# Top-2 experts computed for sorted rows instead of for all rows, beside a recurrent scan

## The reference

```python
xn = layernorm(x)
# L0_attn: a recurrence along the 512 tokens of every sequence
x_norm = layernorm(xn) * g + b;  x_norm += depthwise_conv3(x_norm)
gate, input_gate = split(x_norm @ gate_w.T + gate_b)      # 2 x 128 columns
Bm = x_norm * sigmoid(input_gate) @ B_w.T + B_b           # 64 columns
Cm = x_norm @ C_w.T + C_b
def step(state, bc):                                      # lax.scan, 512 steps
    s = layernorm(state @ A_bar + b_t);  return s, c_t * s
s = (ssm @ D_w.T + D_b) * sigmoid(gate)
# L0_ffn: a dense part and a mixture of 8 experts, of which each row uses 2
abel_out = gelu(xn2 @ abel_w + abel_b)
topw, topi = top_k(xn2 @ moe_gate_w + moe_gate_b, 2);  topw = softmax(topw)
h  = gelu(xn2 @ ew1[e] + eb1[e])                          # 128 -> 256, every e
eo = h @ ew2[e] + eb2[e]                                  # 256 -> 128, every e
moe_out = sum_e eo * w_dense[e];  moe_out = moe_out @ expm(gens[i]) for i in 0, 1, 2
gate = sigmoid(concat(abel_out, moe_out) @ gc_w + gc_b)
ffn = xn + abel_out * (1 - gate) + moe_out * gate
out = x + s * silu(ffn)
```

## Time and profile before

| | us |
|---|---|
| median of 3 runs | 539.81 (539.56 to 542.43) |
| profiled execution, its own time | 543.42 |
| profiled execution, span in the trace | 541.6 |
| front, to the first transpose of the scan | 102.79 |
| scan, 5 rounds | 402.3 (102.79 to 505.10) |
| behind the scan | 36.5 |

### The profile page before, as it was taken

One profiled execution on the slowest core, in us unless ns is written; L12 is line 12 of the kernel. 1 busy time (PEld: TensorE's weight loads), 2 busy tenths in 40 slices (PEclk: granted clock), 3 DMA queues, 4 the chain that ended last, 5 costly groups with the idle time before them and its releaser, 6 DMA issues. The chain is left out here.

```text
span 541.6 us, 13237 instructions
## 1 busy us (share of the span) xinstructions
PE 444.0 (82%) x4780; PEld 343.0 (63%) x4780; DVE 377.2 (70%) x1471; ACT 250.1 (46%) x597; POOL 209.2 (39%) x201
## 2 busy tenths in 40 slices
PE   2866799799889888988898898689889889998247
PEld 1766748477656666676676676567766566776135
DVE  3878579377878587777768676667677576868445
ACT  0325922445455335554455546154645355554420
POOL 2266645012532253243325414332443143425443
PEclk9959959899999798999999999799999799999759
DMA  8200000000000000000000000000000000000004
GB/s 268 79 7 0 2 1 1 2 1 2 2 2 2 1 2 1 1 2 1 2 2 0 3 1 1 2 1 2 1 2 2 1 1 2 2 1 2 0 4 155
DMA packets 6483, 7.65 MB, mean 14 GB/s; under 512 B 2424, under 2 KB 4378, under 8 KB 6426
## 3 DMA queue, kind: packets, MB, share of 16 engines
q1 hardware_dynamic: 5850, 4.77, 2.8%
q10 hardware_dynamic: 576, 2.10, 1.1%
HBM read 4.76 MB, written 2.10 MB: 13 GB/s over the span
## 5 line engine op out<-in xcount | busy, mean ns | idle before, releaser
L1336 POOL TENSOR_TENSOR xpad<-xpad 128x512 f32<-128x512 f32 x64 | 82.8, 1294 | 243.0 <-ACT xpad L1248 187.3
L1157 PE MATMUL bank<-ew,hT 128*128 128x128 f32 x1024 | 143.5, 289 | 0.0
L1248 ACT ACTIVATE xpad<-bank,wd 128x128 f32<-128x128 f32 x256 | 73.1, 369 | 128.4 <-PE bank L1157 128.2
L1157 PEld LDWEIGHTS bank<-ew,hT 128*128 128x128 f32 x1024 | 124.8, 195 | 9.1 <-issue 0.7
L1240 ACT ACTIVATE hT<-bank,eb_col 128x512 f32<-128x512 f32 x128 | 81.2, 687 | 50.7 <-PE bank L194 50.7
L980 PE MATMUL bank<-Mrep,wT 32*32 32x64 f32 x2560 | 69.7, 223 | 36.4 <-DVE wT L886 35.8
L980 PEld LDWEIGHTS bank<-Mrep,wT 32*32 32x32 f32 x2560 | 45.0, 106 | 77.8 <-issue 72.4
L896 DVE SCALAR_TENSOR_TENSOR ring<-bank,Rho,Dv 128x64 f32<-128x64 f32 x124 | 35.2, 284 | 65.1 <-PE bank L980 61.5
L192 PE MATMUL bank<-xf,ew_high 128*128 128x512 f32 x128 | 61.6, 481 | 0.0
L194 PE MATMUL bank<-xf,ew_rest 128*128 128x512 f32 x128 | 52.2, 408 | 0.0
L193 PE MATMUL bank<-xf,ew_high 128*128 128x512 f32 x128 | 52.2, 408 | 0.0
(11 more groups left out here) (288 smaller groups left out, 716.5 us busy)
## 6 DMA issues: line engine op xcount, KB each, us to landing
X<-in_L_attn_x ACTq DMA_DIRECT2D x4, 512.0 KB, 6.1
out<-gi SPq DMA_DIRECT2D x8, 256.0 KB, 2.0
late<-in_L_ffn_ew SPq DMA_DIRECT2D x1, 1024.0 KB, 5.3
pulled<-in_L_ffn_gens SPq DMA_DIRECT2D x1, 192.0 KB
gate_w<-in_L_attn_gate_w SPq DMA_DIRECT2D x1, 128.0 KB, 7.4
D_w<-in_L_attn_D_w SPq DMA_DIRECT2D x2, 32.0 KB, 6.4
abel_in<-in_L_ffn_abel_w SPq DMA_DIRECT2D x1, 64.0 KB, 1.8
bias_in<-in_L_ffn_abel_b SPq DMA_DIRECT2D x3, 0.5 KB
```

The costliest lines, as they stand in the source:

```text
L1157: t = pe.matmul(bE[e % 2][:, s * P:(s + 1) * P], hT[:, e % 2, k, s * P:(s + 1) * P], ew2[:, e, k, :], start=(k == 0), stop=(k == K - 1))
L1248: t = act.activation(scaled[e % 2][:, s, :], bE[e % 2][:, s * P:(s + 1) * P], ACT.Copy, scale=w)
L1336: pool.tensor_tensor(acc, acc, scaled[e % 2], ALU.add).then_inc(sem("added"), 1)
```

## The change

Instead of all 8 experts for all rows, only the two experts of each row are computed.

1. Routing makes places as well as weights: for both halves of the rows (2048 rows, 4096 row-expert pairs each), the pairs are sorted by expert, each expert's rows padded to full tiles of 128. A half has room for 39 tiles, both have 78. `slots` is each pair's place, `expert_of` each tile's expert.
2. GpSimd scatters the normalised rows by `slots` to DRAM: 64 indirect DMAs of 128 rows of 512 bytes (L1487). Later it gathers the results back: 64 indirect DMAs of 128 rows of 516 bytes (L1500). GpSimd has no arithmetic in the scan any more; the sorted buffers are cleared by two DMAs in the front.
3. A tile's weights (both matrices, bias, 581 words on 128 partitions, 297 KB) are copied from `experts` in SBUF to one of five `record` places by a DMA whose source is chosen by a register that SyncE loads (`fetch`, L1524), 78 of them. Rows come in and go out in three chunks per body of 13 tiles.
4. TensorE's program is loops. Round 0 is a loop of 8 turns of 4 steps, which carry `abel_pre`, `gate_pre` and a transposition of the result. Rounds 1 to 3 are 3 x 2 bodies of 16 steps with 13 tiles each: in step i it computes `layer1` of tile i-2, transposes the rows of tile i and computes `layer2` of tile i-3. Round 4 is a loop of 8 turns of 4 steps with three dummy products per step (`keep_warm`).
5. The split into high and rest parts is gone; the expert products are float32. C is projected in step 1 of each body.
6. The mixing of the results moves from GpSimd to VectorE, in given steps of the scan (from step 100 of 160 on, two of the eight tiles behind the scan), with ScalarE making the gains.
7. There is one block instead of three. The work behind the scan starts before the verdict of the check; the fallback would redo it.

```diff
+        HALF_TILES = Q * P * 2 // ROWS + E - 1      # 39
+        BODY = 13
+        experts = sb("experts", [P, E, RECORD])
+        record = sb("record", [P, 5, RECORD])
...
-                def split_tile(n):
-                    pool.wait_ge(sem("zT_used"), n + 1)
-                    split(xf[:, 0, n, :], xf[:, 1, n, :], gi[:, n, :])
...
+            dve.tensor_tensor_scan(places..., restart..., hits..., 0.0, ALU.mult, ALU.add)
...
+                def layer1(b, tile0, u):
+                    ...
+                    for k in range(K):
+                        t = pe.matmul(hidden_bank(u)[:, k * P:(k + 1) * P], w[:, k * P:(k + 1) * P], rows_T[:, u % 2, :], start=True, stop=True)
+                def layer2(b, tile0, u):
+                    ...
+                    for k in range(K):
+                        pe.matmul(o, hidden[:, u % 2, k, :], w[k], start=(k == 0), stop=False)
+                    pe.matmul(o, ones_all3[:, :], bias, start=False, stop=True).then_inc(sem("rows_done"), 1)
+                def keep_warm(times, bank=7):
+                    for i in range(times):
+                        pe.matmul(banks[bank][:, :], ones_all3[:, :], bias_all3[:, 1]..., start=True, stop=True)
...
-                for r in range(ROUNDS):
-                    for k in range(L):
-                        tensor_step(pe, r * PER + k + 1)
-                        n, i = divmod(r * L + k, TILE_STEPS)
-                        for h in range(...):
-                            expert_half(n, h)
+                with pe.Fori(0, NB) as n:
+                    tensor_step(pe, n * 4 + 1)
+                    abel_pre(n)
+                    tensor_step(pe, n * 4 + 2)
+                    gate_pre(n)
+                    tensor_step(pe, n * 4 + 3)
+                    tensor_step(pe, n * 4 + 4)
+                    abel_transposes(n)
+                with pe.Fori(0, 3) as r:
+                    with pe.Fori(0, 2) as h:
+                        for i in range(BODY_STEPS):
+                            tensor_step(pe, turn + (PER + i + 1))
+                            if 2 <= i < BODY + 2: layer1(b, tile0, i - 2)
+                            if i < BODY: rows_transpose(b, tile0, i)
+                            if i >= 3: layer2(b, tile0, i - 3)
+                            if i == 1: C_proj(2, b)
+                            keep_warm(FILL_BODY.get(i, 0))
+                with pe.Fori(0, L // 4) as j:
+                    for i in range(4):
+                        tensor_step(pe, j * 4 + (4 * PER + i + 1))
+                        keep_warm(3)
...
-                    act.copy(acc, bR4).then_inc(sem("sum_started"), 1)      # and scale(e), 8 per tile
+                for b in range(BODIES):
+                    for s in range(BODY_STEPS):
+                        gelus(b, s - 2); rows_transposed(b, s); rows_copied(b, s - 3)
+                        scalar_mix(...)        # ACT_MIX = {91: 0, 98: 1, 105: 2, 113: 3}
...
-                        pool.tensor_tensor(acc, acc, scaled[e % 2], ALU.add).then_inc(sem("added"), 1)
+                            pool.indirect_dma_start(sorted_rows[h], ...slots[:, j, q:q + 1]..., z_rows[:, q, :], None)
+                            pool.indirect_dma_start(pulls[:, n % 3, j, s, :], None, expert_rows[...], ...slots...)
...
+                    e = sp.value_load(expert_of[t:t + 1, h:h + 1], min_val=0, max_val=E - 1)
+                    if before >= 0:
+                        sp.wait_ge(sem("rows_done"), before + 1)
+                    sp.dma_start(record[:, at], experts[:, ds(e, 1), :].squeeze(1)).then_inc(sem(f"record{at}"), 16)
```

More of the change, by code:

```diff
@@ L17 @@
 UNROLL = 8
+ROWS = 128
+HALVES = 2
 SEG = 16
@@ new lines, in layer2 @@
+                def layer2(b, tile0, u):
+                    _, w, _, bias = fields(record[:, RECORD_PLACE[u]])
+                    pe.wait_ge(sem("hidden"), tile0 + (u + 1))
+                    pe.wait_ge(sem("rows_copied_out"), tile0 + (u + 1 + BODY - SINCE[u]))
+                    o = out_bank(u)
+                    for k in range(K):
+                        pe.matmul(o, hidden[:, u % 2, k, :], w[k], start=(k == 0), stop=False)
+                    pe.matmul(o, ones_all3[:, :], bias, start=False, stop=True).then_inc(sem("rows_done"), 1)
@@ new lines, in _ @@
+                gated_ssm(dve, 0, 0)
+                gated_ssm(dve, 0, 1)
+                vector_mix(dve, 6, 3)
+                vector_mix(dve, 6, 4)
+                for part in range(3):
+                    vector_mix(dve, 7, part)
+                gated_ssm(dve, 0, 2)
+                gated_ssm(dve, 0, 3)
+                vector_mix(dve, 7, 3)
+                vector_mix(dve, 7, 4)
+                dve.wait_ge(sem("mixed"), NB)
+                for n in range(4, NB):
+                    gated_ssm(dve, 0, n)
@@ new lines, in _ @@
+                sp.wait_ge(sem("ew2r_ready"), E)
+                sp.wait_ge(sem("eb2_placed"), 16)
+                sp.wait_ge(sem("slots_ready"), 1)
+                sp.wait_ge(sem("tiles_known"), 1)
+                for u in (0, 1, 2, 3, 12):
+                    fetch(u)
+                for c in range(3):
+                    load_rows(0, c)
+                for tile in range(TILES):
+                    b, u = divmod(tile, BODY)
+                    after = tile + (13 if u == 12 else 5 if u >= 8 else 4)
+                    if after < TILES:
+                        fetch(after)
+                    for c, (first, end) in enumerate(CHUNKS):
+                        if u == end - 1:
+                            if b + 1 < BODIES:
+                                load_rows(b + 1, c)
+                            store_rows(b, c)
```

1785 lines of the change are left out of this document (943 added, 842 removed).

## The result

| | us |
|---|---|
| changed kernel, median of 4 runs | 445.94 (438.85 to 459.51) |
| before, beside it | 539.68 (539.32 to 542.43) |
| ratio | 0.812, interval 0.808 to 0.817 |
| profiled execution, time and span | 438.99 and 437.1 |

Forecast were 432 us, measured 445.94; by the medians the kernel is faster by a factor of 1.21. The four runs are two of 439 and two of 453 and 460, and the ratio above (a factor of 1.23) compares the fast ones alone. What separates them is one of the rivals, as the experiments bear out.

A forecast was written before the change was run, and what follows sets the result against it. TensorE's stream in program order was taken as the scan's bound. Start 95.4, round 0 52.6, boundaries 11, bodies 147, crossed waits 19, mixing 15, round 4 49.8, turns 16.5 and end 27.3 gave span 433.6, hence 432 us; range 405 to 455.

The forecast's parts named there:

- The step of 1.57 us: Rounds 1 to 3: TensorE's time for a full scan step with its expert products, about VectorE's 1.55 us.
- Start of the scan: Front of the kernel: GpSimd's slowdowns and idle time removed, VectorE's sorting added, 102.8 us becoming 95.4.
- Round 0 and loop turns: Round 0 takes 52.6 us, including 3.0 of TensorE excess; 25 loop turns at 0.66 us add 16.5.
- Half clock: Rival, 0.12: gaps in rounds 0 and 4 drop TensorE to 1.2 GHz, +26 and +19 us, 477 us.
- Crossed waits: Rounds 1 to 3: steps wait for ScalarE in two places, one in four late by 0.76 us, 19 us.
- mixing 15 us in the bodies: Rounds 2 and 3: four tiles of mixing on VectorE at 4.1 us, 15 of 16.4 us staying on the path.
- Mixing in round 4 and behind the scan: VectorE's mixing of two tiles in round 4, 8.2 us, and two behind the scan, 7.8 us.
- Behind the scan: After the scan: mixing, normalising, check, C, gate, adding and last store take 27.3 us instead of 36.5.
- DMA bound: Rival, 0.14: moving 5.6 MB per body at 182 GB/s takes 31 us against 24.5, +39, 471 us.
- TensorE's loops: Rival, 0.11: nine turns of bodies and outer loops stall TensorE 4 us each, +33, 465 us.
- Indirect DMAs: GpSimd's 64 scatters and 64 gathers cost 1.26 us each, as its 128 x 512 addition, covered by the scan.
- the fourth rival: GpSimd's indirect DMAs decide, 0.08, of which 0.06 slower: above 3.4 us each the kernel is slower; 617 us at 4.

The follow-up runs named there:

- experiment 3: Changed kernel plus one more float32 product of 128 columns behind layer 1 of each of the 78 tiles: 456.01 us, ratio 0.840.
- first job: Four variants of the changed kernel on one chip (no dummies; dummies added in round 0; VectorE's mixing cut; weights' copies cut): 576 to 615 us in every run.
- experiment 6: Two edits of the changed kernel: all eight additions of x on VectorE, median 446.71 us; fallback code left out, 458.71 us.
- third job: On another chip: changed kernel 455.04 us; with dummies added in round 0 438.69; VectorE's mixing cut 429.12; weights' copies cut 447.07.

## Why the prediction was right, and where not

**The total: partly luck.** The two runs at 439 us lie 7 us over the forecast, the median 14. A term of 16.5 us was close to nothing, and the clock, the scan's start and the end cost about as much that had not been priced.

**The bound and the arithmetic: right for the full step.** The step of 1.57 us came out at 1.61, rounds 1 to 3 at 188.0 against 193.5. The added product lengthens a full step by 0.22 us, so there TensorE's stream does bound; the rounds as a whole it does not bound alone (experiment 3). The scan went from 402.3 us to 303.6 with the products for six of eight experts taken out; no run separates that from the other parts of the change.

**Start of the scan: 4.2 us short.** The B projection in front of it ran at a granted clock of 0.50 in the stretch from 87 us on: 31 of its records took 6.82 us, where the trace of before has 3.68 for 32 of the same form. That is about 3.3 of the 4.2 us:

```profile
91.60 6.82 PE L392 MATMUL bank<-B_wT,gi 128*128 128x64 f32 x31
```

The forecast counted VectorE's sorting and no clock.

**Round 0 and loop turns: right in the sum for a wrong reason.** An undisturbed turn took 124.34 - 118.03 = 6.31 us for four steps of 1.55 with the jump back in it: 0.1 us for both, where 0.38 + 0.66 stood. The loop turns' term, 16.5 us in all, was close to nothing; the earlier trace rows, ScalarE's turn without a gap, had said so, and the value was taken from rows of another kind (gaps in front of weight loads, beside which TensorE's products run on). In round 0 its place was taken by the clock: counted from transpose to transpose, the first, second and fifth turn took 8.76, 9.02 and 7.84 us instead of 6.31, and the last, with the boundary, 10.30 instead of the 8.79 of the kernel with dummies. That is 8.2 us, without which the round would have taken 52.9.

**Half clock, a rival at 0.12: it happened in part of the runs.** Priced at 26 us for round 0, it cost up to 22.8 beyond the first profile (83.9 against 61.1), and that profile holds some 8 us of it already. It is not an alternative to the forecast but a state in which the same program is found: median 445.94 in one job, 455.04 in another. The statement "round 0 keeps TensorE three quarters busy" was no reason against it. In round 4, where the forecast saw the same risk, the clock stayed at 0.91 to 1.00 with the dummies in all profiles outside the first job.

**Crossed waits 19 us, mixing 15 us in the bodies: right in the sum, not one by one.** Beyond 24.5 us a body, rounds 1 to 3 took 188.0 - 147 - 6.6 for the boundaries = 34.4 us, where 19 + 15 + 5.9 = 39.9 had been put, 34 of it without the loop turns. Taking VectorE's mixing out gained 0 there. Round 3 is 11 us over round 2, and ScalarE's gains, the mixing and the clock share it in parts that no run separates. The prediction had named the gains ("it is late only when it also makes gains") and priced them at nothing.

**Mixing in round 4 and behind the scan: right**, 9.7 (some of it clock) and 7.7 us against 8.2 and 7.8.

**Behind the scan: 6.6 us short.** VectorE's stretch was 26.3 us. The end was sized by the last store of before, 2.5 us, and measured 7.6. The part that failed is that term: a row of the old end was used for the new one, and what makes the new end 5 us longer is open (experiment 6).

**DMA bound: did not come.** 193 to 213 GB/s moved in rounds 1 and 2 at a share of 0.56 to 0.67, above the 182 of the rival's price, and a ninth of the weights' bytes gained at most 4 us. For stretches of some us the DMA engines are full all the same (0.95 from 177 to 181 us); what that costs lies within the 11.7 us of waits for `record`.

**TensorE's loops: no stall.** The Trainium skill ("Runtime: NRT & Kernel Launch", section "Instruction fetch mechanics") speaks of a fetch at a taken branch to a far target; a turn of round 0 shows no sign of it. In round 1 the gaps in front of the scan's product that the sequencer leaves are 7.2 us in 30 steps, none over 0.8, so the turn between the bodies can't hide 4 us either. Of the two queues that the profile marks "instruction", the one with packets of 16 KB moves three of them from 160 to 191 us and none from 191 to 349, while five of the six bodies run; whose code it carries the profile does not say.

**Indirect DMAs: 1.26 us each, the value taken, by luck**, and on time in three jobs of four, the first comparison included. In the other the kernels were slower than before by 7 to 12%, the sign of the fourth rival, by a mechanism that it did not have: GpSimd kept its pace, the others stood still. The condition given (p above 3.4 us) was not met.

## What to carry to other kernels

Price a state, not only a mean: where TensorE has gaps in a stretch, forecast it at both clock levels, and try some dummy products in its free step before anything else; here 24 of them were worth 16 us beside the changed kernel, and the four runs with them lay within 6 us. When work moves between engines, count the small instructions of the engine that prepares it: seventeen activations per tile take ScalarE 4.9 us, the three operations on VectorE that use them 3 x 1.13 = 3.4. And read an experiment by its stretches, with the clock of each beside it: a total here agreed with a theory that the rounds contradicted, and a "costs nothing" came out of two rounds at different clocks.

The fastest complete kernel with an interval is the changed one with three dummies in the free step of round 0: 438.69 us, ratio 0.809 (0.803 to 0.815). Together with all additions on VectorE it was not tried.

## What the runs showed of the hardware

An indirect DMA of 128 rows of 512 or 516 bytes holds GpSimd for 0.96 us and comes every 1.26. An activation of one column takes ScalarE 0.28 to 0.31 us in a row of them. And while GpSimd issues indirect DMAs, TensorE, VectorE and ScalarE can stand still for up to 49 us at a time on one chip (four kernels of four, at the same places) and not at all on two others. The kernel before, which has no indirect DMA, does not tell the chips apart: it took 541, 540 and 542 us on the three. TensorE's granted clock can stay at 0.50 in a stretch in which it is busy 88 to 93% of the time (changed kernel in the third job, 98 to 140 us), and the same program in another execution has the full clock back in the second turn of the same loop. An addition of 128 x 512 takes VectorE 0.69 us with GpSimd idle and 1.26 beside one on GpSimd.
